# First experts' weights with four neighbouring rows per partition, and a layer norm that writes its features in that order

## The chip, the core and the metric

The kernel runs on one core of one Trainium2 chip. The time is device microseconds (us) from start to end of one execution; the number given is the median of several runs. Before the change it is 1501.26 us (three runs, 1498.11 to 1503.68).

## What is computed

The reference is a graph network of two layers on 1250 nodes with 512 features, each layer with a graph convolution and a block of experts. The change lies in the expert block of the first layer. Cut to what matters:

```python
x2 = layernorm(x, ln2_g, ln2_b).reshape(B * S, H)          # 1250 rows, H = 512
probs = softmax(x2 @ wr)                                    # E = 64 experts
gate_v, gate_i = top_k(probs, 2)                            # two experts for each row
gate_v = gate_v / sum(gate_v)
# each expert takes up to C = 78 rows, in order of the rows
buf = zeros((E, C, H)).at[ef, posc].add(tok)                # tok: rows of x2
h = gelu(einsum('ech,ehf->ecf', buf, w1) + b1)              # w1: 64 x 512 x 256
y = einsum('ecf,efh->ech', h, w2) + b2                      # w2: 64 x 256 x 512
moe_out = sum over the two experts of y[ef, posc] * gate
```

All numbers are 32-bit floats. A product over the 512 features doesn't depend on the order in which they are summed, as long as rows and weights have them in the same order. The change uses this.

## The kernel before

**Stages.** The program is a row of blocks; within a block each engine runs its own list of instructions, and semaphores order them. The stages are: first graph convolution (0 to 281 us), projections (to 400), attention (to 707), `first_router` (to 788), `first_experts` (to 1065), second convolution (to 1276), second router and experts, end. The 1250 rows are ten tiles of 125.

**First router.** The sync engine (SP) first issues gain and shift of the layer norm (line 1092), the router weights `w_r` (line 1094, 128 partitions with 4 pieces of 256 B each) and the weights of the first five experts. TensorE multiplies tile after tile by the output projection (line 1005, eight passes a tile, two PSUM banks in turn). VectorE then does for each tile: the sum with the residual (line 1052), mean and variance (`row_moments`, lines 156 to 158), and for the tile before it the layer norm (`normalize`, lines 170, 174, 176), of which ScalarE forms the root (line 165). The two operations of lines 174 and 176 are (row - mean) * gain and then * 1/std + shift, each over 125 x 512 elements, into `T.rows_a`. TensorE transposes groups of four, four and two tiles from `T.rows_a` (line 129) when they are normed, between the products, and multiplies them by `w_r` for the logits (line 993). When all rows are normed, SP stores `T.rows_a` as `rows0` in HBM, row by row.

**First experts.** 64 experts, one after the other. Per expert:

- SP loads the first weights `ew1` (512 x 256, line 690) and the second weights `ew2` (256 x 512, line 692), 512 KB each, into one of 8 slots; a slot is free when the output of the expert 8 before it is done (`S.ey_done`). The loads stand on SP's queue (q1).
- GpSimd (POOL) copies a column of row numbers (line 1120) and gathers 78 rows of 2 KB from `rows0` by an indirect DMA (line 1127, queue q0) into one of two slots. It waits for the transposes of the expert two before (`S.ex_turned`).
- TensorE does `hidden(r)` (line 1202: 8 products, 16 passes), `turn(r + 1)` (line 1192: four transposes of the next expert's rows, when they are gathered) and `output(r - 1)` (line 1211: 4 passes).
- VectorE empties the transposes (line 1264) and the output (line 1270), ScalarE does the gelu (line 1248) and issues the store of the output to HBM (line 1241, queue q10).

`ew1` is laid out so that partition p of block k holds feature row k * 128 + p: four rows that are 128 rows apart, so four pieces of 1 KB per partition, 512 pieces in all. `ew2` has two pieces of 2 KB per partition.

The block before the second experts loads its weights in the same two manners, nothing else moving beside them: first W1 (4 MB) in pieces of 1 KB, then W2 (4 MB) in pieces of 2 KB.

Of the kernel before, what the change touches and what calls it, by code (L numbers as in the profile page):

```python
# [29 lines left out]
NT = N // P  # L30
# [205 lines left out]
def graph_convolution(nc, T, S, A):  # L236
# [44 lines left out]
    with nc.Block() as block:  # L281
# [52 lines left out]
        def _(dve):  # L334
# [4 lines left out]
            for i in range(PAIRS):  # L339
                dve.wait_ge(S.x_loaded[i], 32)  # L340
                for t in (2 * i, 2 * i + 1):
                    row_moments(dve, link, T, T.x, t, S.z_var)
                for t in (2 * i, 2 * i + 1):
                    dve.wait_ge(S.z_std, t + 1)
                    normalize(dve, link, T, T.rows_a, T.x, t).then_inc(S.z_rows, 1)
# [100 lines left out]
        def _(act):  # L446
# [7 lines left out]
            def roots(i):  # L454
                row_roots(act, T, (2 * i, 2 * i + 1), S.z_var, S.z_std)
# [527 lines left out]
def first_router(nc, T, S, A):  # L983

    with nc.Block() as block:
# [45 lines left out]
        def _(act):  # L1031
            for t in range(NT):
                row_roots(act, T, [t], S.x2_var, S.x2_std)
# [14 lines left out]
        def _(dve):  # L1048
            link = Chain(dve, S.dve_chain, T.dve_at)
            def added(t):  # L1050
# [3 lines left out]
                row_moments(dve, link, T, T.rows_b, t, S.x2_var)  # L1054
# [35 lines left out]
        def _(sp):  # L1090
# [3 lines left out]
            sp.dma_start(T.w_r, A.L0_ffn_wr.rearrange("(k p) e -> p k e", k=KD)).then_inc(S.wr_loaded, 16)  # L1094
# [188 lines left out]
def second_convolution(nc, T, S, A):  # L1283
# [6 lines left out]
    with nc.Block() as block:  # L1290
# [70 lines left out]
        def _(act):  # L1361
# [11 lines left out]
            for t in range(NT):  # L1373
                if t + 1 < NT:
                    counts(t + 1)
                act.wait_ge(S.conv_var, t + 1)
                act.activation(T.std[:, t:t + 1], T.spread[:, t:t + 1], ACT.Sqrt).then_inc(S.conv_std, 1)
# [17 lines left out]
        def _(dve):  # L1395
            link = Chain(dve, S.dve_chain, T.dve_at)

            def add(t):
# [3 lines left out]
                row_moments(dve, link, T, T.x, t, S.conv_var)  # L1402

            def normalized(t):
                dve.wait_ge(S.conv_std, t + 1)
# [31 lines left out]
def second_router(nc, T, S, A):  # L1437

    with nc.Block() as block:
# [41 lines left out]
        def _(act):  # L1481
            row_roots(act, T, range(0, 6), S.f_var, S.f_std)
            copy_group(act, T, T.feats, S, 3, 0, 2, 4)
            row_roots(act, T, range(6, NT), S.f_var, S.f_std)
# [13 lines left out]
        def _(dve):  # L1498
            link = Chain(dve, S.dve_chain, T.dve_at)
            for t in range(NT + 1):  # L1500
                if t < NT:
                    row_moments(dve, link, T, T.x, t, S.f_var)
                if t > 0:
                    dve.wait_ge(S.f_std, t)
# [248 lines left out]
def semaphores_by_name(semaphores):  # L1753
# [9 lines left out]
    S.dve_chain, S.z_var, S.z_std = semaphores("dve_chain z_var z_std")  # L1763
# [19 lines left out]
    S.gates_ready, S.gates_turned, S.x2_var = semaphores("gates_ready gates_turned x2_var")  # L1783
    S.x2_std, S.logits_ready, S.gap_ready = semaphores("x2_std logits_ready gap_ready")
# [243 lines left out]
```

## Time and profile before

| what | value |
|---|---|
| median of three runs | 1501.26 us (1498.11 to 1503.68) |
| the profiled execution | 1498.17 us |
| its span, first to last instruction | 1496.1 us |
| TensorE busy / VectorE busy | 1414.7 us (95%) / 745.7 us (50%) |
| granted TensorE clock, mean over the span | 0.981 |
| first router | 707 to 788 us |
| first experts | 788 to 1065 us |
| DMA moved in the whole run | 142.38 MB |

Times in the rows are us from the start of the span unless marked ns. PE is TensorE's matmul side, PEld its weight load, which runs beside it; DVE is VectorE, ACT ScalarE, POOL GpSimd, SP SyncE, and a q behind a name (SPq) is that engine's sequencer. L1202 is line 1202 of the kernel. An idle time in brackets is the time that the engine stood still just before, with what ended it. `b_r` is any of the large SBUF regions.

### The profile page before, as it was taken

The numbers are of one execution on the slowest core, as the hardware profiler recorded it, in microseconds if no ns is written. First come the engines' busy times: TensorE is split into PE (matmuls) and PEld (weight loads), VectorE is DVE, ScalarE is ACT, GpSimd is POOL, SyncE is SP. The second block draws the span as 40 slices with busy tenths as digits, with TensorE's granted clock in tenths as the row PEclk, the third lists the DMA queues.
The fourth block names the chain that finished last, engine by engine and source line by source line (L and its number), as shares of the span: only waits on it lengthen the run. The fifth ranks groups of instructions, "written<-read, shape, count | busy, mean of one in ns | idle before, by whom it ended". The sixth has DMA issues, their size and how long they took to land. (4 is left out here: it accounts for less than half of the span.)

```text
span 1496.1 us, 24506 instructions
## 1 busy us (share of the span) xinstructions
PE 1414.7 (95%) x7979; PEld 914.2 (61%) x7980; DVE 745.7 (50%) x1549; ACT 461.9 (31%) x1149; POOL 224.8 (15%) x355
## 2 busy tenths in 40 slices
PE   8999999999999999999998999999899999889968
PEld 4688854455477777777555666666445555646642
DVE  6899965661277777776572222222250012533421
ACT  3599930111155555554011111111340012201111
POOL 1133310000000000000213222222420000002225
PEclk9999999999999999999999999999999999789999
DMA  5000000020000000000428999999620000813326
GB/s 152 29 0 0 0 1 0 6 79 0 28 2 2 1 2 2 2 2 11 149 69 253 315 318 328 311 315 315 181 67 0 0 0 0 297 47 117 122 93 190
DMA packets 94059, 142.38 MB, mean 95 GB/s; under 512 B 13285, under 2 KB 50555, under 8 KB 93863
## 3 DMA queue, kind: packets, MB, share of 16 engines
q1 hardware_dynamic: 69297, 97.52, 21.3%
q0 software_dynamic: 14976, 26.81, 6.5%
q10 hardware_dynamic: 9718, 17.12, 3.4%
q8 instruction: 45, 0.74, 0.2%
q14 instruction: 23, 0.19, 0.0%
HBM read 115.09 MB, written 26.29 MB: 94 GB/s over the span
## 5 line engine op out<-in xcount | busy, mean ns | idle before, releaser
L949 DVE TENSOR_REDUCE b_row_max<-ps 125x1 f32<-125x1251 f32 x80 | 116.5, 1456 | 60.3 <-PE ps L848 60.3
L1202 PEld LDWEIGHTS ps<-b_r 128*128 128x128 f32 x1024 | 124.2, 192 | 33.8 <-issue 32.4
L1202 PE MATMUL ps<-b_r 128*128 128x78 f32 x1024 | 122.3, 273 | 1.1 <-DVE b_r L1264 1.1
L1211 PE MATMUL ps<-b_r 128*78 128x512 f32 x256 | 120.3, 593 | 0.0
L576 PE MATMUL ps<-b_r 125*125 125x160 f32 x660 | 118.3, 315 | 0.0
L498 ACT ACTIVATE b_r<-b_r 125x125 f32<-125x125 f32 x330 | 107.6, 389 | 9.3 <-DVE b_r L393 4.9
L1248 ACT ACTIVATE b_r<-ps,b_r 128x78 f32<-128x78 f32 x128 | 34.6, 322 | 229.9 <-PE ps L1202 229.9
L848 PE MATMUL ps<-b_r 64*125 64x417 f32 (+1 forms) x480 | 95.2, 526 | 3.1 <-DVE ps L969 1.2
L882 PE MATMUL ps<-b_r 125*64 125x125 f32 x1600 | 94.7, 272 | 1.1 <-DVE b_r L909 1.1
L1106 POOL TENSOR_TENSOR b_x<-b_x,b_r 125x512 f32<-125x512 f32 x10 | 12.7, 1267 | 544.0 <-DVE b_r L1052 544.0
L576 PEld LDWEIGHTS ps<-b_r 125*125 125x125 f32 x660 | 92.0, 187 | 1.0
L1127 POOL DMA_INDIRECT b_r<-rows,b_ex_ids x88 | 85.5, 971 | 46.3 <-issue 40.9
L114 PE MATMUL ps<-b_ones_bf 125*128 125x512 bf16 x322 | 80.5, 411 | 12.3 <-PEq L1162 4.0
L1264 DVE COPY b_r<-ps 128x312 f32<-128x312 f32 x64 | 30.9, 483 | 119.4 <-PE ps L1192 119.4
L882 PEld LDWEIGHTS ps<-b_r 125*64 125x64 f32 x1600 | 85.3, 136 | 5.9 <-DVE b_r L909 1.0
L594 PE MATMUL ps<-b_r 125*125 125x512 f32 x200 | 86.3, 593 | 2.2 <-POOL b_r L312 2.2
L1120 POOL COPY b_ex_ids<-b_ids 78x1 int32 (+3 forms) x89 | 15.9, 179 | 478.9 <-SPq L1585 238.8
L1270 DVE COPY b_r<-ps 78x512 f32<-78x512 f32 x64 | 44.0, 687 | 83.1 <-PE ps L1211 81.4
L1330 PE MATMUL ps<-b_r 125*128 125x417 f32 (+1 forms) x240 | 84.2, 513 | 0.8 <-ACT b_r L140 0.8
L914 ACT ACTIVATE b_r<-ps 125x500 f32<-125x500 f32 x80 | 46.6, 583 | 112.2 <-PE ps L863 112.2
L312 POOL TENSOR_TENSOR b_r<-b_r 125x160 f32 x110 | 56.0, 509 | 137.2 <-ACT b_r L492 133.0
L398 DVE TENSOR_TENSOR b_r<-ps,b_r 125x480 f32<-125x480 f32 x110 | 71.7, 652 | 0.1
(260 smaller groups left out, 2221.7 us busy)
## 6 DMA issues: line engine op xcount, KB each, us to landing
b_r<-L_ffn_w SPq DMA_DIRECT2D x128, 512.0 KB, 9.7
y<-b_r ACTq DMA_DIRECT2D x64, 156.0 KB
b_r<-L_ffn_W SPq DMA_DIRECT2D x2, 4096.0 KB, 20.0
y<-b_r ACTq DMA_DIRECT2D x24, 256.0 KB, 2.4
rows<-b_r SPq DMA_DIRECT2D x2, 2400.0 KB
b_x<-x SPq DMA_DIRECT2D x5, 480.0 KB
out<-b_x SPq DMA_DIRECT2D x10, 240.0 KB
y<-b_r SPq DMA_DIRECT2D x1, 2048.0 KB, 11.3
```

The lines of the kernel that those rows point to most:

```text
L114: pe.matmul(T.ps[:, bank, :].rearrange("p (t e) -> p t e", t=4), ones, ones.unsqueeze(1).to_broadcast([P, 4, 128]), start=True, stop=True)
L398: dve.tensor_tensor(T.cells[:, b], cell_iota.unsqueeze(1).to_broadcast([EC, CJ, WC]), column(T.cell_col, g, WC), ALU.is_equal).then_inc(S. ...
L498: last = act.activation(T.weighted[:, i % 2, j, :], T.sources[:, i % 2, j, :], ACT.Copy, scale=T.w_col[:, bass.ds(g0 + i, 1), j])
L576: last = pe.matmul(T.ps[:P, 2 + b, 0:WC], T.weighted[:, b, j, :], T.cells[:, b, j, :], start=(j == 0), stop=(j == CJ - 1))
L594: last = pe.matmul(T.ps[:P, t % 2, :], T.at[:, k, t * P:(t + 1) * P], T.rows_a[:, k, :], start=(k == 0), stop=(k == NT - 1))
L848: last = pe.matmul(T.ps[:P, 3 * h + c, 0:width], T.qt[b:b + DH, m, t * P:(t + 1) * P], T.kt[b:b + DH, m, c0:c0 + width], start=True, stop= ...
L882: last = pe.matmul(T.ps[b:b + DH, bank_of((VALUES, n)), 0:P], T.v[:, k, m * 128 + b:m * 128 + b + DH], T.probs_t[:, n % 2, h, k * P:(k + 1 ...
L949: link(dve.tensor_reduce(T.row_max[:, slot:slot + 1], T.ps[:P, 3 * h:3 * h + 3, 0:CW], AX.XY, ALU.max))
L1127: pool.indirect_dma_start(slots[:parts, r % 2, :], None, rows, bass.IndirectOffsetOnAxis(ap=T.ex_ids[:parts, r % 4:r % 4 + 1], axis=0))\
L1202: last = pe.matmul(T.ps[:, 2 + r % 2, f * CAP:(f + 1) * CAP], T.ew1[r % WS][:, k, f * 128:(f + 1) * 128], T.ex_t[:, r % 2, k, :], start=(k ...
L1211: last = pe.matmul(T.ps[:CAP, 4 + r % 2, :], T.eh[:, r % 2, f, :], T.ew2[r % WS][:, f, :], start=(f == 0), stop=(f == FK - 1))
L1330: last = pe.matmul(T.ps[:, j % 8, 0:n], T.rows_a[:, k, m * 128:(m + 1) * 128], T.ct_f[:, k, c0:c0 + n], start=(k == 0), stop=(k == NT - 1))
```

## The change

Three access patterns change, and one helper is added.

- `ew1`: partition p now holds the feature rows 4p to 4p + 3, which lie next to each other in HBM: one piece of 4 KB per partition, 128 pieces in all. In the tile, block k then holds the features 4p + k.
- `w_r` is loaded in the same manner: one piece of 1 KB per partition where there were four of 256 B.
- the layer norm of the first router writes feature 4p + k to column k * 128 + p of the row, so that the transposes bring it to partition p of block k. The new `normalize_by_fours` reads the rows and gain and shift in their order, and writes with a step of 128 elements; its second operation also reads with that step. The stored and gathered rows have the new order as well.
- the pairs of semaphores for variance and root of four stages become one pair that counts on (0, 10, 20, 30 at the start of a stage). Order and number of the waits stay as they are.

```diff
-def row_roots(act, T, tiles, var_ready, std_ready):
+def row_roots(act, T, S, use, tiles):
     for t in tiles:
-        act.wait_ge(var_ready, t + 1)
-        act.activation(T.std[:, t:t + 1], T.spread[:, t:t + 1], ACT.Sqrt).then_inc(std_ready, 1)
+        act.wait_ge(S.rows_var, use * NT + t + 1)
+        act.activation(T.std[:, t:t + 1], T.spread[:, t:t + 1], ACT.Sqrt).then_inc(S.rows_std, 1)
+
+def by_fours(row):
+    return row.rearrange("q (p k) -> q p k", k=KD)
+
+def normalize_by_fours(dve, link, T, out, rows, t, gain, shift):
+    turned = out[:, t, :].rearrange("q (k p) -> q p k", k=KD)
+    link(dve.reciprocal(T.rstd[:, t:t + 1], T.std[:, t:t + 1]))
+    link(dve.scalar_tensor_tensor(out=turned, in0=by_fours(rows[:, t, :]), scalar=T.moments[:, t, 0:1], in1=by_fours(gain),
+                                  op0=ALU.subtract, op1=ALU.mult))
+    return dve.scalar_tensor_tensor(out=turned, in0=turned, scalar=T.rstd[:, t:t + 1], in1=by_fours(shift),
+                                    op0=ALU.mult, op1=ALU.add)
...
 def load_expert(sp, T, S, A, e, slot):
-    sp.dma_start(T.ew1[slot], A.L0_ffn_w1[bass.ds(e, 1)].rearrange("o (k p) f -> p (o k) f", k=KD))\
+    sp.dma_start(T.ew1[slot], A.L0_ffn_w1[bass.ds(e, 1)].rearrange("o (p k) f -> p (o k) f", k=KD))\
       .then_inc(S.ew_loaded[slot], 16)
...
             def normalized(t):
-                dve.wait_ge(S.x2_std, t + 1)
-                normalize(dve, link, T, T.rows_a, T.rows_b, t, T.affine[:, 2, :], T.affine[:, 3, :])\
+                dve.wait_ge(S.rows_std, 1 * NT + t + 1)
+                normalize_by_fours(dve, link, T, T.rows_a, T.rows_b, t, T.affine[:, 2, :], T.affine[:, 3, :])\
                     .then_inc(S.x2_rows, 1)
...
-            sp.dma_start(T.w_r, A.L0_ffn_wr.rearrange("(k p) e -> p k e", k=KD)).then_inc(S.wr_loaded, 16)
+            sp.dma_start(T.w_r, A.L0_ffn_wr.rearrange("(p k) e -> p k e", k=KD)).then_inc(S.wr_loaded, 16)
```

## Rows read from the trace of the kernel before

**Rows 1.** The page: busy tenths of the 16 DMA engines, 40 equal slices.

```profile
DMA  5000000020000000000428999999620000813326
```

**Rows 2.** Windows, expert stage: stretch, length, busy us of each engine, clock, DMA.

```profile
core 0: us, PE busy (x) PEld busy (x) DVE busy (x) ACT busy (x) POOL busy (x), PEclk, DMA share, GB/s
...
800.00:840.00 40.00, 37.81 (x228) 25.80 (x227) 11.48 (x20) 4.87 (x18) 11.44 (x20) 1.00 1.07 329
840.00:1040.00 200.00, 187.80 (x1148) 129.68 (x1147) 55.61 (x96) 25.97 (x96) 54.92 (x96) 1.00 1.05 317
```

**Rows 3.** Waits from 790 to 1050 us, then SP's: total us, times, longest.

```profile
PEld ps L1192 <- DMA b_r<-rows,b_ex_ids: 20.6, 45, 1.2
...
PE ps L1192 <- DMA b_r<-rows,b_ex_ids: 15.3, 38, 1.1
...
SPq L690 <- PE ps L1211: 20.2, 11, 3.1
```

**Rows 4.** Timeline of TensorE, 1039 to 1049 us: start, length, instructions.

```profile
1039.89 1.91 PE L1202 MATMUL ps<-b_r 128*128 128x78 f32 x16
...
1043.62 1.91 PE L1202 MATMUL ps<-b_r 128*128 128x78 f32 x16
...
1048.28 0.90 PE L1202 MATMUL ps<-b_r 128*128 128x78 f32 x7
```

**Rows 5.** Gathers, DMA view, from 800:840, 840:1040, 1046:1048, 1380:1450: count, median landing.

```profile
b_r<-rows,b_ex_ids POOLq DMA_INDIRECT x10, 6.9
...
b_r<-rows,b_ex_ids POOLq DMA_INDIRECT x48, 6.9
...
b_r<-rows,b_ex_ids POOLq DMA_INDIRECT x1, 6.8
...
b_r<-rows,b_ex_ids POOLq DMA_INDIRECT x13, 3.4
```

**Rows 6.** Timeline, one turn: transposes, then the gather that waits for them.

```profile
883.29 0.49 PE L1192 MATMUL ps<-b_ident,b_r 78*128 78x78 f32 x4 [0.41 <-DMA b_r<-rows,b_ex_ids]
...
884.75 0.97 POOL L1127 DMA_INDIRECT b_r<-rows,b_ex_ids  x1 [0.54 <-issue]
```

**Rows 7.** Queues of SP and POOL, 840:1040: packets, MB, share of 16 engines.

```profile
q1 hardware_dynamic: 36651, 48.05, 79.4%
q0 software_dynamic: 3075, 7.68, 13.4%
```

**Rows 8.** Windows in the load before the second experts: 1 KB, then 2 KB pieces.

```profile
1281.00:1289.00 8.00, 6.84 (x47) 4.90 (x45) 7.47 (x26) 2.81 (x9) 0.00 (x0) 0.96 1.09 350
1291.00:1299.00 8.00, 7.32 (x47) 7.09 (x46) 1.57 (x6) 2.53 (x5) 0.00 (x0) 0.71 1.04 387
```

**Rows 9.** VectorE's groups by line: busy us, mean ns; idle before.

```profile
L174 DVE SCALAR_TENSOR_TENSOR b_r<-b_r,b_moments,b_affine 125x512 f32<-125x512 f32 x10 | 7.5, 752 | 0.4
...
L158 DVE TENSOR_SCALAR b_spread<-b_moments 125x1 f32<-125x1 f32 x10 | 1.5, 153 | 0.3
...
L764 DVE TENSOR_REDUCE b_rdeg<-b_r 125x1250 f32<-125x12500 uint16 x1 | 21.5, 21454 | 2.0 <-PEq L281 2.0
...
L949 DVE TENSOR_REDUCE b_row_max<-ps 125x1 f32<-125x1251 f32 x80 | 116.5, 1456 | 60.3 <-PE ps L848 60.3
```

**Rows 10.** Timelines of TensorE and VectorE in the first router.

```profile
714.86 20.84 PE L1005 MATMUL ps<-b_w_b,b_r 128*125 128x512 f32 x48 [0.54 <-DMA b_w_a<-L_ffn_wr]
...
760.20 1.07 PE L129 MATMUL ps<-b_ident,b_r 125*128 125x125 f32 x8 [0.78 <-DVE b_r L176]
...
741.23 0.69 DVE L1052 TENSOR_TENSOR b_r<-ps,b_r 125x512 f32<-125x512 f32 x1 [2.02 <-PE ps L1005]
...
748.15 0.69 DVE L1052 TENSOR_TENSOR b_r<-ps,b_r 125x512 f32<-125x512 f32 x1 [3.46 <-PE ps L1005]
...
755.02 0.69 DVE L1052 TENSOR_TENSOR b_r<-ps,b_r 125x512 f32<-125x512 f32 x1
...
759.39 0.75 DVE L176 SCALAR_TENSOR_TENSOR b_r<-b_r,b_rstd,b_affine 125x512 f32<-125x512 f32 x1
```

More of the change, by code:

```diff
@@ L1032, in _ @@
             for t in range(NT):
-                row_roots(act, T, [t], S.x2_var, S.x2_std)
+                row_roots(act, T, S, 1, [t])
                 for g in groups_after(t):
@@ L1401, in add @@
                 dve.wait_ge(S.moe_added, t + 1)
[L1402 removed]
+                row_moments(dve, link, T, T.x, t, S.rows_var)
             def normalized(t):
[L1405 removed]
+                dve.wait_ge(S.rows_std, 2 * NT + t + 1)
                 normalize(dve, link, T, T.rows_a, T.x, t).then_inc(S.conv_rows, 1)
@@ L1481, in _ @@
         def _(act):
-            row_roots(act, T, range(0, 6), S.f_var, S.f_std)
+            row_roots(act, T, S, 3, range(0, 6))
             copy_group(act, T, T.feats, S, 3, 0, 2, 4)
-            row_roots(act, T, range(6, NT), S.f_var, S.f_std)
+            row_roots(act, T, S, 3, range(6, NT))
             for g in range(1, len(GROUPS)):
@@ L1501, in _ @@
                 if t < NT:
-                    row_moments(dve, link, T, T.x, t, S.f_var)
+                    row_moments(dve, link, T, T.x, t, S.rows_var)
                 if t > 0:
-                    dve.wait_ge(S.f_std, t)
+                    dve.wait_ge(S.rows_std, 3 * NT + t)
                     normalize(dve, link, T, T.rows_b, T.x, t - 1).then_inc(S.f_rows, 1)
@@ L1762, in semaphores_by_name @@
     S.prep_done, S.prep_transposed, S.columns_ready = semaphores("prep_done prep_transposed columns_ready")
-    S.dve_chain, S.z_var, S.z_std = semaphores("dve_chain z_var z_std")
+    S.dve_chain, S.rows_var, S.rows_std = semaphores("dve_chain rows_var rows_std")
     S.z_rows, S.z_done, S.z_copied = semaphores("z_rows z_done z_copied")
@@ L1782, in semaphores_by_name @@
     S.counted, S.placed, S.table_made = semaphores("counted placed table_made")
-    S.gates_ready, S.gates_turned, S.x2_var = semaphores("gates_ready gates_turned x2_var")
-    S.x2_std, S.logits_ready, S.gap_ready = semaphores("x2_std logits_ready gap_ready")
+    S.gates_ready, S.gates_turned = semaphores("gates_ready gates_turned")
+    S.logits_ready, S.gap_ready = semaphores("logits_ready gap_ready")
     S.gap_exp, S.rows0_stored = semaphores("gap_exp rows0_stored")
@@ L1794, in semaphores_by_name @@
     S.conv_relu, S.conv_done, S.conv_normed = semaphores("conv_relu conv_done conv_normed")
-    S.conv_added, S.conv_turned, S.conv_var = semaphores("conv_added conv_turned conv_var")
-    S.conv_std, S.bn_var, S.bn_root = semaphores("conv_std bn_var bn_root")
+    S.conv_added, S.conv_turned = semaphores("conv_added conv_turned")
+    S.bn_var, S.bn_root = semaphores("bn_var bn_root")
     [S.bn_ready] = semaphores("bn_ready")
@@ L1803, in semaphores_by_name @@
     S.b11_loaded, S.f_rows, S.rows1_stored = semaphores("b11_loaded f_rows rows1_stored")
-    S.logits1_done, S.f_var, S.f_std = semaphores("logits1_done f_var f_std")
+    [S.logits1_done] = semaphores("logits1_done")
     S.logits1_ready, S.rx_ids_ready, S.rx_turned = semaphores("logits1_ready rx_ids_ready rx_turned")
```

11 lines of the change are left out of this document (5 added, 6 removed).

## The prediction

> **What bounds the kernel now.** I read the page first [rows 1]. TensorE is busy nearly everywhere, but a busy TensorE is not one at its peak, so that says little. What stands out in the line of the DMA engines (40 slices of 37.4 us each) are the slices from about 790 to 1045 us, where all 16 are busy at nine tenths or more: the stage of the first 64 experts. The change touches that stage and the one before it (the first router), so I cut the expert stage out by windows [rows 2]. There the DMA share is 1.05 to 1.07 (records overlap a little, so more than 1 means full), at 317 to 329 GB/s, and TensorE is busy for 188 of 200 us at a granted clock of 1.00.
>
> Next I asked what TensorE waits for in that stage [rows 3]. It never waits for expert weights. It waits for the gathered rows that line 1192 transposes: 20.6 us in the weight-load rows and 15.3 us in the matmul rows. Those two overlap and must not be added. The sync engine, which issues the weights, waits for a free slot in only 11 of its 56 turns in the loop [rows 3].
>
> The order of TensorE's work shows what such a wait costs [rows 4]. From one expert's hidden product to the next (line 1202) it takes 3.73 us when the rows are there (1039.89 to 1043.62), and 4.66 us when they are late. The mean is 200/48 = 4.17 us, since 48 gathers start in the 200 us from 840 [rows 5]. So 0.44 us per expert is waiting.
>
> What sets 4.17? The rows have two slots. The gather for an expert starts when the transposes of the expert two before are done. From the start of those transposes (883.29) to the gather's start (884.75) it is 1.46 us [rows 6]; the gather then takes 6.9 us to land [rows 5]. Two steps are 1.46 + 6.9 = 8.36 us, one is 4.18. This agrees with 4.17, so **the loop is bound by the landing time of the gather**, and a step moves by half of what that time moves. Without the stream of weights beside it, in the second expert stage, a larger gather of the same kind lands in 3.4 us [rows 5]. So some 3.5 us of the 6.9 is time spent beside other transfers. That is where this change acts.
>
> Are the weights a limit as well? The weights' queue moved 48.05 MB in the 200 us [rows 7]. An expert has 1.049 MB, so the queue delivers one in 4.36 us, while one is used in 4.17. The queue falls behind by 0.19 us per expert, about 11 us over 58, and the lead of up to 8 slots covers it. That is why nobody waits for it.
>
> **The change part by part.** *1. Four neighbouring rows per partition.* The first weights of an expert go from 512 pieces of 1 KB to 128 pieces of 4 KB. The bytes, the number of transfers and the slots stay. The trace has no 4 KB pieces on this queue, so I work them out. In the load before the second experts, 1 KB pieces run at share 1.09 and 350 GB/s, and 2 KB pieces at share 1.04 and 387 GB/s [rows 8]. Per piece of one engine that is 16 x 1.09/350 x 1024 = 51 ns and 16 x 1.04/387 x 2048 = 88 ns. The straight line through both gives 162 ns for 4 KB, an estimate. Per expert and engine: 32 x 51 = 1.63 us before, 8 x 162 = 1.30 us after, so 0.33 us of engine time less, or 0.31 us at the share of 1.05. The queue could then deliver an expert in 4.05 us.
>
> By itself this saves nothing, because TensorE doesn't wait for weights: 0.19 of the 0.31 us only stops the queue from falling behind. What counts is whether the gather lands sooner, and the bounds lie on both sides of nothing. The gather's 39 packets of 4 KB are 2 to 3 on each engine (7.68 MB in 48 gathers [rows 7]), and between them the engine serves the weights. (a) If it serves a whole transfer's share of the weights at each turn, a turn over first weights shrinks from 1.63 to 1.30 us: the landing gains 0.33 us. (b) If it serves one piece at each turn, each of 3 packets waits for 162 instead of 51 ns: the landing loses 0.33 us on an engine that is at first weights. A step moves by half, and 58 gathers run beside the weights (10 from 800 to 840 and 48 after), so the bounds are -9.6 and +9.6 us. I take 0. The nearest row is the last gather, which starts at 1047.0 when the queue carries only 2 KB pieces, and lands in 6.8 us against 6.9 for the mix of 1 and 2 KB [rows 5]: the size of the pieces, so far as it varies here, doesn't show.
>
> *2. Layer norm in the matching order.* The two operations of 512 elements (lines 174 and 176, 752 ns each, ten times each; the row of the first stands in [rows 9]) now write with a step of 128 elements, and the second also reads so: three stepped streams per tile. No row shows a stepped write. The nearest row is the reduction of line 764, which reads with a step of 1250 elements: (21454 - 153)/12500 = 1.70 ns per element, against (1456 - 153)/1251 = 1.04 for the plain reduction of line 949 (153 ns is a one-element operation) [rows 9]. That is 0.66 x 512 = 0.34 us for one stepped stream. The bounds per tile are 0 and 3 x 0.34 = 1.02 us. I take 0.34, the read alone, since only a read has a row.
>
> How many tiles lie on the path? TensorE's eight passes of line 1005 for a tile take 20.84/6 = 3.47 us, and VectorE's round takes 3.44 (from tile 7's sum at 748.15 to tile 9's at 755.02, halved), so both are at the bound [rows 10]. VectorE idles twice, before 741.23 (2.02 us) and before 748.15 (3.46 us), while TensorE transposes and forms logits. These gaps swallow the extra time of tiles 4 and 5. The other eight pass on: tiles 0 to 3 hold up the transposes that follow the first six products at 714.86 + 20.84 = 735.70, tiles 6 to 9 the last transposes at 760.20, which start 0.06 us after VectorE's last operation ends (759.39 + 0.75) [rows 10]. So 8 x 0.34 = +2.7 us, with bounds 0 and +8.2.
>
> The Trainium skill (SBUF — State Buffer, Specifications (TRN2)) has a rule that speaks against this part: SBUF is read in 16-byte lines, full rate needs at least two accesses to a line, and a step to a new line costs. The line 764 row agrees in direction. By that rule every stepped stream would pay, which is the upper bound of 8.2 us.
>
> *3. Router weights (w_r).* 512 pieces of 256 B become 128 of 1 KB. TensorE waits 0.54 us for this load at the start of the router [rows 10]. Landing earlier gives between 0 and 0.54 us; I take -0.3.
>
> *4. The semaphores.* Eight become two that count on over the stages. The waits stand at the same places and the stages are apart, so they queue nothing behind anything new: 0. Transposes, gathers, stores of rows and all products keep shape and number: 0.
>
> **The sum.** 0 + 2.7 - 0.3 + 0 = +2.4 us. The profiled execution took 1498.17 us, of which 1496.1 are the span and 2.07 lie around it; it would become 1500.6. It lies 3.1 us below the median of the three runs, 1501.26, so for the median I forecast 1503.7.
>
> **The rivals.** *The queue is relieved and the gather profits.* For it: the DMA share of 1.05, and 0.33 us per expert less work. Against: the queue stays full for most of the stage, and the gather landed no sooner from 800 to 840 (6.9 us), though the queue was then less backed up. If the step follows the queue's new rate, 58 x (4.17 - 4.05) = -7.0 us, so 1496.7; by (a) -9.6, so 1494.1. With a gather that is never late the step would be 3.73: -25.5, so 1478.2, the floor.
>
> *Large pieces hold up the gather: slower.* Each engine takes turns between queues; a turn over first weights gets longer when the pieces are four times as long. By (b) the step grows by 0.17 us: 1503.7 + 9.6 = 1513.3. If a turn is up to 16 pieces it goes from 16 x 51 = 0.82 to 8 x 162 = 1.30 us, so the landing loses 0.48 us and the time is 1503.7 + 13.9 = 1517.6. It decides from a landing of about 7.2 us on: half of 0.3 us, 58 times, is 8.7 us. For it: the gather waits 3.5 us beside the queue, far more than its own 3 packets take. Against: the last gather of [rows 5].
>
> The Trainium skill (DMA: Bandwidth & Descriptors, Queues, rings and completion order) says that an engine goes round its queues packet by packet, with about 9 to 17 descriptors to a packet. By that rule the turns of the case with 16 pieces would hold, and the change would lose. By that rule, too, the last gather of [rows 5], beside 2 KB pieces alone, should have landed later than the others; the trace doesn't bear that out.
>
> *VectorE's steps cost in full.* Three streams pay, the router becomes VectorE's, +8.2 - 0.3: 1509.2.
>
> *The change doesn't do what it says*, and the 4 KB are cut into the old pieces: part 1 is then 0 for sure, and the time is the forecast's.
>
> **How the numbers follow.** The forecast, with the cut pieces inside it, gets 0.40, at 1503.7, and with part 2 between its bounds 1501 to 1509. The relieved queue gets 0.30, the held-up gather 0.25, VectorE in full 0.05. A kernel of this kind can be told from no change at about 0.5%, 7.5 us: faster is below 1493.8, slower above 1508.8. The relieved queue is below 1493.8 if part 2 is cheap or the gather gains more than 0.33 us, which I think likely enough to put nearly all of its 0.30 there: faster 0.28. Slower is the held-up gather and VectorE in full: 0.30. That leaves 0.42. The range leaves out the floor and the far end of the held-up gather: 1485 to 1518.
>
> **What would show it.** Part 1: the landing time of the gather in 840 to 1040 (6.9 now), the number of 48 gathers in 200 us, the weights' queue with about half as many packets; a mean of about 162 ns for 4 KB pieces. The relieved queue: landing at 6.6 or less and sync engine waits for slots. The held-up gather: landing at 7.2 or more, and more than 36 us of waits on it. Part 2: the two operations at 752 and about 1090 ns; anything else moves its term, and the gaps before 741 and 748 us get smaller. Part 3: no wait of line 1005 on w_r. The prediction is wrong if the gather's landing moves by more than 0.3 us.

## The result and the profile after

The changed kernel took 1508.16 us (median of 20 runs, 1500.29 to 1518.65), the kernel before beside it 1501.07 (20 runs, 1495.69 to 1506.6). The ratio is 1.0053, 95% interval 1.0036 to 1.0071: slower by 0.5%, some 7 us. Ratios here and below leave out two executions, of 1801 and 1814 us, that fell into a slower state of the chip. The forecast was 1503.7 in a range of 1485 to 1518. The profiled execution took 1506.69 us, of which 1505.0 are its span.

Lines move by 15 in the changed kernel: 1005 is now 1020, 1192 is 1207, 1202 is 1217, 1211 is 1226, 690 is 705; the two operations of the layer norm (174 and 176) are 177 and 179. I read the same views in the same order as before. First the page's row of the DMA engines, 40 slices:

```profile
DMA  5000000110000000002227999999420000723326
```

It looks like [rows 1], so the expert stage is as full and about as long as it was. Cut out by windows (stretch, length, busy us of each engine, clock, DMA share, GB/s; the last is the first transposes in the router):

```profile
800.00:840.00 40.00, 37.91 (x227) 27.26 (x226) 10.27 (x18) 5.41 (x20) 10.48 (x19) 0.91 1.01 324
840.00:1040.00 200.00, 186.65 (x1139) 128.79 (x1138) 55.62 (x96) 25.45 (x94) 54.74 (x95) 1.00 1.03 324
736.94:740.34 3.40, 3.40 (x17) 3.40 (x18) 3.23 (x7) 1.63 (x4) 1.26 (x1) 0.51 0.00 0
```

From 840 to 1040 us the DMA share is 1.03 where [rows 2] have 1.05, at more GB/s (324 for 317). From 800 to 840 us the granted clock is 0.91, where it was 1.00. That is not the change's alone: with nothing but the merged semaphores, further down, it is 0.96 in the same window. The DMA view of 840 to 1040 us (queue: packets, MB, share; loads and gathers: count, KB, median landing), then the waits from 790 to 1050 us (total us, times, longest):

```profile
q1 hardware_dynamic: 19705, 49.69, 78.5%
b_r<-L_ffn_w SPq DMA_DIRECT2D x96, 512.0 KB, 9.3
b_r<-rows,b_ex_ids POOLq DMA_INDIRECT x48, 6.9
```

```profile
PEld ps L1207 <- DMA b_r<-rows,b_ex_ids: 18.9, 38, 1.1
PE ps L1207 <- DMA b_r<-rows,b_ex_ids: 14.9, 38, 0.9
...
SPq L705 <- PE ps L1226: 175.9, 56, 5.6
```

The weights' queue has half the packets [rows 7]. An expert load lands in 9.3 us; in the same view of the kernel before it is 12.0. The sync engine now waits for a free slot in all 56 turns, 175.9 us in sum, where it was 20.2 us in 11 turns [rows 3]. So the weights' queue really was relieved. And TensorE got nothing of it: 48 gathers in 200 us, landing in 6.9 us, as in [rows 5], and nearly the same waits for them. The loss is in the router. TensorE there, and VectorE's two operations by line (busy us, mean ns, idle before):

```profile
713.22 20.84 PE L1020 MATMUL ps<-b_w_b,b_r 128*125 128x512 f32 x48 [0.89 <-DMA b_w_a<-L_ffn_wr]
...
736.94 3.54 PE L129 MATMUL ps<-b_ident,b_r 125*128 125x125 f32 x16 [2.88 <-DVE b_r L179]
...
759.24 1.93 PE L129 MATMUL ps<-b_ident,b_r 125*128 125x125 f32 x16 [1.48 <-DVE b_r L179]
...
765.66 1.07 PE L129 MATMUL ps<-b_ident,b_r 125*128 125x125 f32 x8 [2.12 <-DVE b_r L179]
```

```profile
L177 DVE SCALAR_TENSOR_TENSOR b_r<-b_r,b_moments,b_affine 125x512 f32<-125x512 f32 x10 | 11.2, 1116 | 0.4
L179 DVE SCALAR_TENSOR_TENSOR b_r<-b_r,b_rstd,b_affine 125x512 f32<-125x512 f32 x10 | 11.1, 1107 | 0.4
```

Both operations went from 752 [rows 9] to about 1110 ns: 0.72 us per tile, not 0.34. From the first product to the last transposes it is 765.66 - 713.22 = 52.44 us, where it was 760.20 - 714.86 = 45.34 [rows 10]: **7.1 us more, about the size of the whole result**. The spans of the two profiled executions differ by 1505.0 - 1496.1 = 8.9 us, so the rest of the kernel, which varies from one execution to the next, adds 1.8 us here. The first and second transposes of the kernel before, from the same view:

```profile
735.83 1.93 PE L129 MATMUL ps<-b_ident,b_r 125*128 125x125 f32 x16
...
755.11 1.93 PE L129 MATMUL ps<-b_ident,b_r 125*128 125x125 f32 x16
```

Taken piece by piece: first transposes 23.72 us after the first product, before 20.97: +2.75. To the second transposes 22.30, before 19.28: +3.02. To the third 6.42, before 5.09: +1.33. The second piece has a wait of 1.48 us that wasn't there, and 1.54 us that are no wait: the first transposes took 3.54 us instead of 1.93, at a granted clock of 0.51 (last window above), the lower of the two levels, 1.2 GHz. So 5.56 us are waits on VectorE, which 8 tiles x 0.72 = 5.8 us explain, and 1.5 us are the clock, which fell right after TensorE had stood still for 2.88 us.

### The profile page after: what moved, and what is told of

It is laid out like the page before. It is cut to its first block and busy times, and to the rows that moved or that the text cites. A ratio compares the mean times of both kernels' runs of the same rounds, so it can differ in the third digit from the quotient of the medians.

```text
span 1505.0 us, 24506 instructions
## 1 busy us (share of the span) xinstructions
PE 1419.8 (94%) x7979; PEld 918.3 (61%) x7980; DVE 752.1 (50%) x1549; ACT 462.1 (31%) x1149; POOL 224.7 (15%) x355
```

## The experiments

My theory after this reading: the stepped layer norm makes the whole loss, and the large pieces are worth nothing while the gather bounds the loop. The rivals: the merged semaphores cost something; the pieces give back part of the loss, or cost part of it; the pieces have a use that the gather hides. The router column is the time from the first product of line 1005 to the last transposes, in the profiled execution. The step is the mean over 58 experts of the loop, from the fourth to the 62nd hidden product, in the same execution. The clock is the mean granted clock of the whole kernel, averaged over all executions that the ratio uses; for the kernel before it is given for the executions beside the others, on three chips. Of the kernel before, the ratio is 1.

| kernel | ratio, 95% interval | router, us | step, us | slot waits of SP, us (turns) | clock |
|---|---|---|---|---|---|
| before | 1 | 45.34 | 4.180 | 20.2 (11) | 0.9763 to 0.9771 |
| the change | 1.0053, 1.0036 to 1.0071 | 52.44 | 4.199 | 175.9 (56) | 0.9740 |
| the change again | 1.0076, 1.0048 to 1.0105 | 52.43 | 4.260 | 178.6 (56) | 0.9745 |
| semaphores only | 0.9997, 0.9978 to 1.0016 | 45.33 | 4.124 | 104.5 (42) | 0.9775 |
| 4 KB weights only | 1.0014, 0.9977 to 1.0051 | 45.33 | 4.244 | 176.2 (56) | 0.9741 |
| layer norm and w_r only | 1.0102, 1.0059 to 1.0145 | 52.22 | 4.176 | 32.7 (19) | 0.9712 |
| the same again | 1.0099, 1.0072 to 1.0127 | 52.42 | 4.159 | 23.5 (16) | 0.9718 |
| one stepped operation | 1.0004, 0.9973 to 1.0035 | 47.51 | 4.061 | 171.3 (56) | 0.9759 |
| stepped transposes | 1.0049, 1.0028 to 1.0071 | 45.59 | 4.248 | 179.7 (56) | 0.9759 |
| before, gather 3 ahead | 0.9972, 0.9955 to 0.9990 | 45.33 | 4.091 | 2.5 (4) | 0.9758 |
| the change, gather 3 ahead | 0.9967, 0.9941 to 0.9993 | 52.47 | 3.882 | 46.2 (20) | 0.9730 |
| stepped transposes, gather 3 ahead | 0.9940, 0.9920 to 0.9959 | 45.59 | 3.920 | 158.0 (56) | 0.9739 |
| one stepped operation, gather 3 ahead | 0.9898, 0.9870 to 0.9925 | 47.55 | 3.776 | 118.3 (48) | 0.9762 |

**4 KB weights alone.** The kernel before, with the new layout of the first weights only. The rows keep their old order, so the hidden products pair each feature with another one's weights; amount and shape of the work are those of the kernel before.

```diff
-    sp.dma_start(T.ew1[slot], A.L0_ffn_w1[bass.ds(e, 1)].rearrange("o (k p) f -> p (o k) f", k=KD))\
+    sp.dma_start(T.ew1[slot], A.L0_ffn_w1[bass.ds(e, 1)].rearrange("o (p k) f -> p (o k) f", k=KD))\
```

> The kernel before with one edit: the first weights come as 4 KB pieces. The layer norm and the router weights stay as they were, so the experts multiply weights in an order that doesn't match their rows; their work is the same in kind and number. Theory A (the whole loss is the layer norm's stepped writes in the router; the loop is bound by the gather, which doesn't notice the size of the pieces): same as before, within 3 us; 48 gathers in 200 us, landing 6.9 us; waits of the sync engine for slots grow from 20 to over 150 us. Rival B (large pieces hold up the gather): 3 us or more slower, landing above 7.0. Rival C (the relieved queue gives a gain that the layer norm hides in the full change): 3 us or more faster, landing 6.7 or less.

Measured: 1.0014 (0.9977 to 1.0051), nothing that can be told from no change. The waits of its loop, 790 to 1050 us:

```profile
PEld ps L1192 <- DMA b_r<-rows,b_ex_ids: 22.6, 47, 0.9
PE ps L1192 <- DMA b_r<-rows,b_ex_ids: 17.1, 43, 0.8
```

TensorE waits for the gather as in [rows 3], at the same relieved queue as the full change (176.2 us of slot waits). The trace has no landing time for the gathers of this run; 47 of them start in the 200 us from 840. The recorded theory stands, but the interval is wide: it excludes a gain of more than 0.2% and a loss of more than 0.5%, no less.

**The layer norm and w_r alone.** The changed kernel, with the first weights loaded in 1 KB pieces again; here too the hidden products pair features with other features' weights.

> The changed kernel with the first weights back in 1 KB pieces; the stepped layer norm and the new order of the router weights stay. The experts' products mix features, their work is the same in kind and number. Theory A: all of the loss is here, 7 us slower than before, the router 7 us longer, the two operations 1.1 us each. Rival B: only about 4 us slower (the rest comes with the large pieces). Rival C: 9 us or more slower.

Measured: 1.0102 (1.0059 to 1.0145), 13 to 15 us, more than the full change and more than the 7 us of my theory; it is the third of the outcomes written down before. In its router the three pieces are as long as in the full change (52.22 us in all). But later in that stage the clock was low a second time, during the products for the logits (line, then window):

```profile
768.26 9.35 PE L1008 MATMUL ps<-b_w_a,b_r 128*125 128x64 f32 x48
```

```profile
768.26:778.00 9.74, 9.74 (x52) 9.44 (x51) 0.00 (x0) 1.11 (x5) 0.00 (x0) 0.55 0.87 208
```

In the full change the same 48 products took 5.35 us. That is 4 us more in this one execution. To see whether it was chance I ran it again later, beside the full change and the semaphores alone.

**Both again, on one chip, with the semaphores alone.** The last is the kernel before with the merged pairs and nothing else.

> The change with the first weights in 1 KB pieces again. It gave 1.010 where the full change gave 1.005. My theory: the pieces are worth nothing by themselves, the difference is how long the clock stays down in the router in one execution or another, and beside each other the two now give the same ratio within 0.003. The rival: the 4 KB pieces return about 0.005 of what the layer norm loses (the full change 1.005, this one 1.010 again).

> The changed kernel again, beside the next one on the same chip: ratio 1.005. If the clock in the router depends on the wait of 2.9 us before the transposes of tile 0 to 3, it falls there again, for a few us or longer.

> The kernel before with nothing but the merged semaphores. My theory has the whole loss in the stepped layer norm: ratio 1.000 within 0.003, a router of 45.3 us from the first products to the last transposes, a wait of up to 1 us on w_r. The rival is that the merged semaphores carry part of the loss (then the ratio is 1.003 to 1.005).

Measured: 1.0099 (1.0072 to 1.0127), 1.0076 (1.0048 to 1.0105), 0.9997 (0.9978 to 1.0016). The semaphores cost nothing: that rival falls. The ratio of the layer norm alone stayed at 1.010.

The long low stretch didn't come back in its profiled execution, but that says little of the others: the profiled one was the fastest (1507.13 us, clock 0.976), the other four took 1510 to 1519 us at 0.968 to 0.973. The clock column has the mean of all executions. The missing share of the clock times the span is 34.4 us for the kernel before on this chip, 38.5 for the change, 42.6 for the layer norm alone; in the first comparison it was 34.8 and 43.6. The mean times differ by 12 us for the change and by 12 and 13 us for the layer norm alone. So a lower clock can make up to 4 us of the first, and up to 8 or 9 us of the others. This is an upper estimate, since TensorE isn't the bound everywhere. Nor does it belong to the layer norm only: the 4 KB weights alone have 0.9741 beside 0.9768, at no measurable loss. Where in the unprofiled executions the clock falls isn't on record. First transposes of the change again, then of the layer norm alone again:

```profile
738.95 3.02 PE L129 MATMUL ps<-b_ident,b_r 125*128 125x125 f32 x16 [2.85 <-DVE b_r L179]
```

```profile
739.91 3.08 PE L129 MATMUL ps<-b_ident,b_r 125*128 125x125 f32 x16 [2.84 <-DVE b_r L179]
```

The wait of some 2.85 us and the slow transposes behind it are in each of the five profiled executions that have the layer norm with two stepped operations. Whether the 4 KB pieces give back 0.2 to 0.5% beside it stays open. Both pairs point that way (1.0053 and 1.0102; 1.0076 and 1.0099), but the intervals of each pair overlap, the pieces alone (1.0014) don't show it, and in these profiles the step is no shorter with them: 4.199, 4.260, 4.244 against 4.180, 4.124, 4.176, 4.159. In both pairs the full change also has the higher clock of the two (0.9740 for 0.9712, 0.9745 for 0.9718).

**Which stepped stream costs.** One execution of the kernel before, with the two operations of the layer norm in another form in each tile: written, read, or both with a step, with two tensors as inputs or one (line 186 and 189). Its normed rows are not the layer norm's.

```diff
+    n, s = as_far, far
+    pair = [
+        (lambda: two(n(o, 4), s(r, 4), n(gain, 4)), lambda: two(n(o, 4), n(r, 4), s(gain, 4))),
+        (lambda: two(s(o, 4), n(r, 4), n(gain, 4)), lambda: two(s(o, 4), s(r, 4), n(gain, 4))),
+        (lambda: two(s(o, 4), s(r, 4), s(gain, 4)), lambda: two(n(o, 4), n(r, 4), n(gain, 4))),
...
```

> One look at the price of stepped access on VectorE. In the kernel before, the two layer norm operations of each of the ten tiles are replaced by operations on 125 x 512 elements that differ in what is stepped, so the rows that the experts get are not the reference's. Tiles 0 to 2 have two inputs: tile 0 steps one input, then the other; tile 1 steps the output, then output and first input; tile 2 steps all three, then none. Tiles 3 and 4 have one input: output stepped, input stepped, both, none. Tiles 5 to 9 have steps of 2, 4 and 8 elements. Theory A1 (every operation with any stepped stream pays once, about 0.36 us with two inputs): all stepped forms of two inputs 1.1 us, none 0.75. Rival (each stream pays): one 1.1, two 1.45, three 1.8 us. Rival (only writes pay): stepped reads 0.75. With one input the price of the plain operation is 0.55 us and a stepped one 0.9.

Its one time was 1521.98 us, which says little, since the forms differ from tile to tile.

The line's view, cut to one tile each (ns: least, median, most; with two instructions, least and most are the two):

```profile
L186 DVE SCALAR_TENSOR_TENSOR b_r<-b_r,b_moments,b_affine x2: 1112/1114/1116, 723.7 to 724.8; 125x512 f32<-125x512 f32 x2
L186 DVE SCALAR_TENSOR_TENSOR b_r<-b_r,b_moments,b_affine x2: 1108/1114/1121, 727.8 to 728.9; 125x512 f32<-125x512 f32 x2
L186 DVE SCALAR_TENSOR_TENSOR b_r<-b_r,b_moments,b_affine x2: 751/1000/1249, 731.9 to 733.1; 125x512 f32<-125x512 f32 x2
...
L189 DVE TENSOR_SCALAR b_r<-b_r,b_moments,b_rstd x2: 801/806/812, 735.7 to 736.6; 125x512 f32<-125x512 f32 x2
L189 DVE TENSOR_SCALAR b_r<-b_r,b_moments,b_rstd x2: 546/702/858, 739.2 to 740.1; 125x512 f32<-125x512 f32 x2
L189 DVE TENSOR_SCALAR b_r<-b_r,b_moments,b_rstd x2: 547/548/548, 746.5 to 747.0; 125x512 f32<-125x512 f32 x2
L189 DVE TENSOR_SCALAR b_r<-b_r,b_moments,b_rstd x2: 742/745/748, 753.4 to 754.2; 125x512 f32<-125x512 f32 x2
```

Tile 0 reads one input with a step of 128 elements, the first input in one operation and the gain in the other: about 1114 ns. Tile 1 writes with the step in one and writes and reads with it in the other: 1108 and 1121. Tile 2 has all three stepped, 1249, and none, 751. So **the operation pays once, 0.36 us, whether one stream is stepped or two**; the third adds 0.14. With one input it is 546 plain, about 806 with either stream stepped (tile 3) and 858 with both (tile 4). Tile 5 has a step of 2 elements (8 bytes), 547 and 548: free. Tile 6 has a step of 4 elements (16 bytes): 742 and 748.

The same execution has another wait of TensorE before its first transposes, with the clock behind it at the lower level for a part of them (2.58 us for 1.93):

```profile
737.44 2.58 PE L129 MATMUL ps<-b_ident,b_r 125*128 125x125 f32 x16 [2.08 <-DVE b_r L189]
```

**Only one operation stepped.** The changed kernel, whose first operation writes plainly into the place of the next tile, and whose second turns the order.

```diff
-    link(dve.scalar_tensor_tensor(out=turned, in0=by_fours(rows[:, t, :]), scalar=T.moments[:, t, 0:1], in1=by_fours(gain),
+    straight = out[:, t + 1, :] if t + 1 < NT else T.w_b[:P, 0, :]
+    link(dve.scalar_tensor_tensor(out=straight, in0=rows[:, t, :], scalar=T.moments[:, t, 0:1], in1=gain,
                                   op0=ALU.subtract, op1=ALU.mult))
-    return dve.scalar_tensor_tensor(out=turned, in0=turned, scalar=T.rstd[:, t:t + 1], in1=by_fours(shift),
+    return dve.scalar_tensor_tensor(out=turned, in0=by_fours(straight), scalar=T.rstd[:, t:t + 1], in1=by_fours(shift),
```

> The changed kernel, but the layer norm's first operation writes plain rows into the place of the next tile (for the last tile into the used weights of the output projection), and only the second writes with the step of 128 elements; it reads plainly. Theory A with the loss in proportion to the stepped operations: the first operation back at 752 ns, the second still about 1110, so 0.36 us per tile less; VectorE then holds TensorE up too little to let its clock fall; time 3 to 4.5 us above before, half of the full change's loss or a little less. If the loss came from the fallen clock or from the weights alone it would stay at 7 us or go to nothing.

Measured: 1.0004 (0.9973 to 1.0035). The two operations by line, then TensorE in the router:

```profile
L178 DVE SCALAR_TENSOR_TENSOR b_r<-b_r,b_moments,b_affine x9: 750/752/752, 725.7 to 760.1; 125x512 f32<-125x512 f32 x9
L180 DVE SCALAR_TENSOR_TENSOR b_r<-b_r,b_rstd,b_affine x9: 1095/1115/1123, 726.5 to 760.9; 125x512 f32<-125x512 f32 x9
```

```profile
716.54 20.84 PE L1021 MATMUL ps<-b_w_b,b_r 128*125 128x512 f32 x48 [1.09 <-DMA b_w_a<-L_ffn_wr]
...
738.58 1.93 PE L129 MATMUL ps<-b_ident,b_r 125*128 125x125 f32 x16 [1.21 <-DVE b_r L180]
...
758.44 1.93 PE L129 MATMUL ps<-b_ident,b_r 125*128 125x125 f32 x16 [0.71 <-DVE b_r L180]
...
764.05 1.07 PE L129 MATMUL ps<-b_ident,b_r 125*128 125x125 f32 x8 [1.31 <-DVE b_r L180]
```

The router is 2.2 us longer than before instead of 7.1, near the 8 x 0.36 = 2.9 us of one stepped operation per tile. After a wait of 1.21 us the clock didn't fall (1.93 us for the transposes), and the mean clock of all executions is near that of the kernel before (0.9759 for 0.9768). The loss as a whole is no longer measurable: 0.6 us where I expected 3 to 4.5, which still lie inside the interval. The router is not the only difference, though: in this profiled execution the loop is shorter too, at a step of 4.061, the shortest of all versions with two slots, which is 6.9 us in 58 experts, and no run shows why. So the experiment shows that 5 of the router's 7 us, and the fall of the clock in it, go with one of the two stepped operations. That the ratio returns to 1 is more than these 5 us explain.

**The gather one expert further ahead.** If the large pieces have a use that the gather hides, it must show once the gather is out of the way. The rows get four slots, and the gather waits for the transposes of the expert three before. With 1 KB pieces (the kernel before with merged semaphores) and with the full change:

```diff
-        wait_count(pool, turned, q, 4, r - 1)
+        wait_count(pool, turned, q, 4, r + 1 - ahead)
...
-                wait_count(pe, S.ex_loaded[r % 2], q, 8 * WS, 16 * (r // 2 + 1))
+                wait_count(pe, S.ex_loaded[r % 4], q, 4 * WS, 16 * (r // 4 + 1))
```

> The kernel before (with the merged semaphores of the change, since no semaphore is left otherwise), and four slots for gathered rows in place of two, of which three are used ahead: the gather for an expert waits for the transposes of the expert three before, one step earlier. Theory A (the loop is bound by the landing of the gather, and behind it by the weights' queue at 1 KB pieces): the gather has one more step, so its waits go; the step is then set by the queue, 4.2 to 4.36 us less what the eight slots cover, so the loop gains 5 to 12 us at most and TensorE begins to wait for weights. If the loop were bound by TensorE, nothing changes.

> The changed kernel with the gather three ahead. Theory A: the loop can go faster than with 1 KB pieces, since the queue now delivers an expert in 4.05 us or less instead of 4.36: a step of 4.0 to 4.05, 8 to 12 us less than the changed kernel; against the version with 1 KB pieces and the same gathers the loop is 3 to 10 us shorter, which is what the large pieces are worth once the gather isn't the bound. Rival (TensorE's own 3.73 us is the next bound): 25 us less. Rival (the pieces never matter): the same gain as with 1 KB pieces.

Measured: 0.9972 (0.9955 to 0.9990) and 0.9967 (0.9941 to 0.9993), the second in spite of the router's 7.1 us. Of the loop, with 1 KB pieces first and then with 4 KB: the waits from 790 to 1050 us.

```profile
SPq L705 <- PE ps L1226: 2.5, 4, 1.1
...
PEld ps L1217 <- DMA b_r<-L_ffn_w: 5.3, 5, 1.5
...
PEld ps L1207 <- DMA b_r<-rows,b_ex_ids: 0.2, 1, 0.2
```

```profile
SPq L705 <- PE ps L1226: 46.2, 20, 2.8
...
PEld ps L1217 <- DMA b_r<-L_ffn_w: 3.1, 4, 1.1
...
PEld ps L1207 <- DMA b_r<-rows,b_ex_ids: 0.5, 1, 0.5
```

And the weights' queue from 840 to 1020 us, in the same order:

```profile
q1 hardware_dynamic: 33890, 44.42, 80.9%
```

```profile
q1 hardware_dynamic: 18720, 47.17, 77.1%
```

The wait for the gather is gone in both, from some 20 us to under 1. With 1 KB pieces the hidden products now wait for weights, and the sync engine hardly ever for a slot: the queue delivers an expert in 180 x 1.049/44.42 = 4.25 us, and is the bound. With 4 KB pieces it delivers one in 180 x 1.049/47.17 = 4.00 us. The step falls to 4.091 and 3.882. So the large pieces do something, **but only once the gather no longer bounds the loop**.

**The turn of the order on TensorE.** Instead of the layer norm, the transposes pick every fourth column, in the router and in the expert loop; the rows keep their order. Without and with the gather ahead.

```diff
-                                rows[:, t, k * 128:(k + 1) * 128], T.ident[:P, :P])
+                                rows[:, t, :].rearrange("q (p k) -> q k p", k=KD)[:, k, :] if fours else
+                                rows[:, t, k * 128:(k + 1) * 128], T.ident[:P, :P])
```

> First weights and router weights in pieces of four neighbouring rows, layer norm and stored rows in the plain order as before: TensorE picks every fourth column (a step of 16 bytes) when it loads the rows for the transposes, 40 times in the router and 4 times for each expert. Theory A: the loss of the layer norm goes; if the stepped weight load costs TensorE nothing, the time is that of before within 3 us. If it costs as much as on VectorE (a factor of 1.5 on 141 ns, 8 loads an expert), 0.6 us is added to each pair of steps' chain at most, up to 15 us slower.

> The same with the gather three ahead: large pieces, plain layer norm, and the gather's wait gone. Theory A: faster than before by 8 to 14 us and the fastest of the four, since it has the queue's relief without the layer norm's price, if the stepped weight loads of TensorE are cheap; TensorE has 0.3 us per step to spare for them. If the stepped loads cost 0.5 us per expert or more, it is no better than the changed kernel with the gather three ahead.

Measured: 1.0049 (1.0028 to 1.0071) and 0.9940 (0.9920 to 0.9959). The transposes of the gathered rows, by line from 850 to 1000 us, in this kernel and then in the kernel before:

```profile
L1193 PE MATMUL ps<-b_ident,b_r 78*128 78x78 f32 x140 | 24.3, 296 | 4.7 <-DMA b_r<-rows,b_ex_ids 4.0
L1193 PEld LDWEIGHTS ps<-b_ident,b_r 78*128 78x128 f32 x140 | 19.6, 213 | 8.7 <-DMA b_r<-rows,b_ex_ids 6.9 <-issue 1.4
```

```profile
L1192 PE MATMUL ps<-b_ident,b_r 78*128 78x78 f32 x144 | 17.6, 245 | 9.2 <-DMA b_r<-rows,b_ex_ids 8.7
L1192 PEld LDWEIGHTS ps<-b_ident,b_r 78*128 78x128 f32 x144 | 12.1, 141 | 13.8 <-DMA b_r<-rows,b_ex_ids 12.3 <-issue 1.3
```

The router is only 0.25 us longer. In the loop the four transposes of an expert take 4 x 51 ns longer and hold the slot so much longer. The trace shows it: from the start of the transposes to the start of the next gather the median is 1.67 us, against 1.45. That is 0.1 us per step by the arithmetic of the prediction, 6 us over 58 experts, which fits the 1.0049; but the 4 KB weights alone had the same step (4.244) without it, so it isn't shown that this makes the loss. With the gather ahead the slot time is covered, and the kernel beats the one before. The stepped transposes are not free there either: TensorE hardly waits any more, and nearly every step is its own work, 3.92 us where it is 3.73 with plain transposes [rows 4].

```profile
1030.56 1.91 PE L1218 MATMUL ps<-b_r 128*128 128x78 f32 x16
...
1034.48 1.91 PE L1218 MATMUL ps<-b_r 128*128 128x78 f32 x16
```

The 0.19 us are about the 4 x 51 ns, and 11 us over 58 experts.

**Together.** One stepped operation and the gather ahead.

> The full change with the first operation of the layer norm plain (one stepped operation in place of two) and the gather issued three experts ahead over four slots. Expected from the runs with either alone: the full change with the gather ahead gave 0.9967, the plain first operation takes some 4 us off it, so 0.994 (0.992 to 0.996), about the same as the version that steps the transposes. The rival: the gain of a gather ahead holds no longer when VectorE's part is different; then 0.997.

Measured: 1483.69 us, 0.9898 (0.9870 to 0.9925), the fastest of all, **1% below the kernel before** and better than I expected (0.992 to 0.996). Its window from 840 to 1020 us, the gathers of that stretch (count, median landing), and the sync engine's waits from 790 to 1050:

```profile
840.00:1020.00 180.00, 180.00 (x1155) 127.36 (x1154) 56.67 (x97) 26.35 (x98) 55.52 (x98) 1.00 1.03 353
```

```profile
b_r<-rows,b_ex_ids POOLq DMA_INDIRECT x49, 6.7
```

```profile
SPq L706 <- PE ps L1227: 118.3, 48, 6.6
```

TensorE is busy all the time; the step of 3.776 us is near the 3.73 of an expert whose rows are there [rows 4]. The gather still takes 6.7 us to land; nobody waits for it. The step is shorter than with the full change ahead (3.776 against 3.882, 6.2 us in 58 experts), but that is not the gain beyond the expected: the first three experts took 4.6 us longer here (15.03 us from the first to the fourth hidden product, against 10.43), at a clock that was low from 797.6 us for 10.2 us. From the first hidden product to the 62nd the two profiled executions differ by 1.6 us only. The slow start helps to explain why the weights had more lead (118.3 us of slot waits against 46.2): with the full change ahead, the step was 3.73 for some 30 experts and about 4 from then on. Where the rest of the gain comes from stays open; there is one profile of each. The slot waits differ between near-identical kernels as well: 104.5 us with the semaphores alone, 20.2 before.

## Where the prediction was right and wrong

**The bound of the loop: right.** The landing time of the gather set the step. It stayed at 6.9 us when the weights' pieces grew, the step stayed (4.199 for 4.180), and when the gather was issued earlier the step fell. (The first of the slices that I counted as nine tenths full, 785 to 823 us, reads 8 in [rows 1]; nothing hangs on it.)

**Part 1, taken at nothing: right for the time, too large for the engine time.** I had 0.33 us of engine time less per expert. The queue's records give (3200 us are 16 engines for 200 us) 0.794 x 3200/48.05 = 52.9 us of engine time per MB before [rows 7] and 0.785 x 3200/49.69 = 50.6 after, so 2.3 x 1.049/16 = 0.15 us per expert. The straight line through 1 and 2 KB made the 4 KB pieces too cheap. The DMA records of the two traces, sorted by size, show it from 840 to 1040 us: 55.0 ns for a piece of 1 KB and 208.9 for one of 4 KB, against the 51 and 162 of the prediction (2 KB: 105.2 before, 101.2 after, against 88). What I wrote of the relieved queue, that it "saves nothing, because TensorE doesn't wait for weights", is what happened; its sign, the sync engine's waits for slots, appeared in full, but the landing didn't follow. (The sign is a weak one: the merged semaphores alone, with 1 KB pieces, gave 104.5 us of such waits in one execution.) The rival of the relieved queue and the rival of the held-up gather both fall, with 6.9 us (7.0 in the change again) against the 6.6 and 7.2 that they needed. The Trainium skill (DMA: Bandwidth & Descriptors, Queues, rings and completion order) has engines go round their queues by packets of about 9 to 17 descriptors. By my estimate from that rule, 0.48 us in the prediction, pieces four times as long should have delayed the gather by some half a microsecond; the runs don't bear that out.

**Part 2: the mechanism and the count right, the size wrong. This is the step that failed.** Eight tiles on the path, VectorE's gaps swallowing tiles 4 and 5: as described. Two details were not: three groups of transposes were held up and not two, since tiles 6 and 7 hold up the second group and 8 and 9 the last; and of the gaps, the first grew (2.02 to 2.98 us), because TensorE came late itself, while the second shrank (3.46 to 2.72). But I priced a tile at 0.34 us, "the read alone, since only a read has a row". It cost 0.72, because the first operation, which only writes with a step, pays as much as the second. The price of one stepped stream came out near (0.34 forecast from line 764, 0.36 measured), in part by luck: line 764 reads 16-bit numbers from SBUF and line 949 32-bit ones from PSUM, so the two differ in more than the step, and with one input a stepped stream costs 0.26. The rule for putting it together was wrong both ways. It isn't one read per tile (0.34), nor three streams (1.02), but one price per operation. 8 x 0.72 = 5.8, within the bounds of 0 to 8.2 and 3.1 above the value I took. The Trainium skill (SBUF — State Buffer, Specifications (TRN2)), by which SBUF gives full rate only with two accesses or more to a 16-byte line, agrees with the forms in its threshold: a step of 8 bytes is free, one of 16 bytes costs (547 and 745 ns). That each stepped stream pays for itself was my reading of it, and is not what the forms show.

**A term that I didn't have: the clock.** When TensorE had stood still for 2.88 us in front of the first transposes, the clock was granted at the lower level for 3.4 us, which cost 1.5 us more. I had counted a wait on VectorE as its own length only. Over all executions the mean clock of the versions with two stepped operations is lower than before (0.9712 to 0.9745 for 0.9763 to 0.9771). With the layer norm alone that is up to 8 or 9 us, far more than the 1.5 us of the one stretch; with the full change it can't be told apart from what the 4 KB weights have by themselves (0.9741).

**Part 3: wrong sign, small.** TensorE waits 0.89 us for w_r instead of 0.54. With the old layout and the semaphores merged it waited 2.04 us in one execution, so this wait varies by more than the term is worth.

**Part 4: right,** 0.9997.

**The sum.** In place of +2.7 - 0.3 = +2.4 us it should have been 5.6 + 1.5 = 7.1, for a median of about 1508.4; 1508.16 was measured. That it agrees so closely is partly luck: the same kernel again was 1.0076, some 11 us slower than the kernel before, with the same 7.1 us in the router. I had called a change within 0.5% the likeliest; the ratio of 1.0053 is just beyond, on the slower side, and the case that comes nearest to it is the one of VectorE's steps in full (1509.2), to which I gave 0.05. Its time was near, its reason (three streams, a router that is VectorE's throughout) half right. It was worth more than 0.05: "no row shows a stepped write" was a reason to take the middle of the bounds, not the lower of the two prices.

## What to carry to other kernels

Price a stepped access per instruction, not per tensor, and don't take a write for free because only a read has a row. Ask of a faster transfer who waits for it: here the relieved queue was real and worth nothing until the gather, the actual bound, was issued one expert earlier, and then it became part of a gain of 1%. If data has to change its order somewhere, put the one stepped instruction where the engine has slack, and let every other instruction stay plain. And compare the mean clock of all executions, not only of the profiled one: the part of a loss that lies in the clock can be missing from the one trace.

## What the runs showed of the hardware

- VectorE on 125 x 512 f32: with two tensor inputs 751 ns plain, 1108 to 1121 with one or two streams at a step of 128 elements (two of them being the written and the read), 1249 with three; with one input 546, 801 to 812, 858. A step of 2 elements costs nothing (547 and 548 ns), one of 4 costs 0.2 us with one input (742 and 748).
- TensorE's transposes of 78 rows from every fourth column: 296 ns for 245, their weight load 213 for 141. With nothing else in the way that made a step of 3.92 us for 3.73.
- The lower clock came with the wait of 2.84 to 2.88 us in all five profiled executions that had it, and with one of 2.08 us in the same place; with 1.21 and 1.23 us there it didn't come.
- A gather of 39 packets landed in 6.7 to 7.0 us (medians of the runs that have it on record) beside 1, 2 and 4 KB pieces alike, and also with the gather issued one expert earlier, when the weights' queue moved up to 10% more (52.92 MB in 200 us for 48.05).
- A piece of the weights' queue took 55 ns of an engine at 1 KB, 101 to 105 at 2 KB and 209 at 4 KB in the full expert loop, so nearly in proportion to its size (55, 51 to 53 and 52 ns per KB).
